# A graph layer with a feed-forward stage: neighbour sums in one burst per block, four groups of 32 nodes side by side, and every sixth product on VectorE

## The chip, the cores and the metric

The kernel runs on 1 core of one Trainium2 chip. The time is the device time of one execution in microseconds (us), from launch to the last output. Two runs of the kernel before were timed.

## What is computed

`x` has 6250 nodes of 512 values; `src` and `dst` are 106,250 edges (both directions of 50,000, and one loop for each node), sorted by `dst`. The weights of the feed-forward stage are ternary in groups of 128 with a scale each.

```
xn  = layernorm(x)
agg = segment_sum(xn[src], dst, 6250)
h   = xn @ W_self + b_self + (agg / max(deg, 1)) @ W_neigh
h   = layernorm(h) * gamma + beta
h   = where(h >= 0, h, alpha * h)
x1  = x + h + xn
x1n = layernorm(x1)
hid = silu(x1n @ wq_gate.T) * (x1n @ wq_up.T)      # wq: ternary, scale per group of 128
out = x1 + hid @ wq_down.T
```

## The kernel before

Nodes are taken in 49 blocks of 128. There are two stages.

**Prologue.** For each block ScalarE normalises `x`, TensorE turns it (`turn0`) and multiplies it with W_neigh (`product`), and the result is stored to a table in HBM as two fp16 halves, 2 KB a node. Beside this the ternary weights are made (VectorE compares, POOL subtracts, L737), and the range of edges of each block is found on VectorE (`edge_ranges`, with large `hit` tiles and a reduction over partitions on POOL), spread over the blocks from `RANGES_FROM` = 9 on.

**Main stage.** A hand-written schedule of slots, one for each block, and 18 ticks in each. In slot t:
- POOL gathers the table rows of the edges of block t: 18 indirect DMAs (`STEPS`), each 128 edges, 256 KB, into a ring `rows` of 18 tiles (L759). A tile is free again when its sum has run (`p_used`).
- VectorE builds `hot`, a matrix of ones for edge against node for 18 x 128 edges and 128 nodes (L1293), and counts edges per node from it (L1303, three reductions).
- TensorE sums: for each of the 18 tiles two matmuls of 512 columns (`sum_step`: L889 and L891, high and low half) with `hot` as the weights, into `agg_ps`. The table `AGG_AT` spreads them over ticks 2 to 17, between the matmuls of the feed-forward stage. `degree` (L877, one column) runs at tick 6.
- VectorE and ScalarE finish the block: mean, two layer norms, slope (`norms`, in slots t+1 and t+2); SyncE turns it by DMA for the feed-forward stage.

**Feed-forward work** runs in the same slots. Blocks are taken in chunks: one block, then 12 chunks of 4 blocks (512 columns). A step is one group of 128 inputs: two matmuls (L994, L995, high and low half) into one of 6 banks `f_ps`. Because each group has its own scale, the bank is multiplied in place by a ratio between two steps of one sum (a "product", L1088 on ScalarE, L1432 on VectorE). The six banks take turns. A chunk of four blocks has 132 steps and 106 products. `own` steps (x @ W_self in fp32, L807, four for each of the later blocks) stand in the same list and weigh two steps each. `PACE` says how many steps go into a slot: 38, and 35 (`EVEN`) in the last 11 slots. A chunk does not start before its last block is ready: chunk c at slot 4c + 3.07. Before slot 49 all products are ScalarE's; after it VectorE takes two of five.

In the first five slots 23 blocks more are multiplied by W_self (`held_part`), each with a load and a store of 256 KB.

Each engine runs its list in order. What an instruction waits for holds everything behind it on that engine.

Of the kernel before, what the change touches and what calls it, by code (L numbers as in the profile page):

```python
# [23 lines left out]
PER_LOAD = 2  # L24
LOADS = STEPS // PER_LOAD
TICKS = 18
BIG = float(1 << 17)
# [9 lines left out]
def build(nc, x, src, dst, W_self, b_self, W_neigh, gamma, beta, alpha, w_gate, w_up, w_down, out):  # L37
# [8 lines left out]
    PASS = STEPS * P  # L46
    EP = 125
# [57 lines left out]
    PACE, EVEN = 38.0, 35.0  # L105
# [62 lines left out]
    AGG_AT = [[] for _ in range(TICKS)]  # L168
    for j in range(STEPS):
        AGG_AT[2 + j * (TICKS - 2) // STEPS].append(j)  # L170

# [36 lines left out]
    room = [(t, k) for t in range(BLOCKS + 8) for k in ((12, 17) if t < BLOCKS else (2, 11))]  # L208
# [53 lines left out]
    src_pad = nc.dram_tensor("src_pad", (E + PASS,), I32, kind="Internal").ap()  # L262
    dst_pad = nc.dram_tensor("dst_pad", (E + PASS,), F32, kind="Internal").ap()

    with ExitStack() as ctx:
# [9 lines left out]
        rows = sb("rows", [P, STEPS, 2 * D], F16)  # L275
# [9 lines left out]
        hot = sb("hot", [P, 2, P, STEPS], F16)  # L285
        node_j = sb("node_j", [P, P, STEPS], F16)
# [4 lines left out]
        idx = sb("idx", [P, 2, STEPS], I32)  # L291
        dstv = sb("dstv", [P, 2, STEPS], F32)
        dstl = sb("dstl", [P, STEPS], F16)
        identf = sb("identf", [P, P], F32)
        ident = sb("ident", [P, P], F16)
# [6 lines left out]
        top = sb("top", [P, BLOCKS], F32)  # L302
        st6p = sb("st6p", [P, 6], F32)
# [12 lines left out]
        rangem = sb("rangem", [P, 2 * BLOCKS], F32)  # L316
        rangei = sb("rangei", [P, 4 * BLOCKS + 1], I32)
        most = sb("most", [P, 1], F32)
        padi = sb("padi", [P, STEPS], I32)
# [10 lines left out]
        idx_o = sb("idx_o", [P, STEPS], I32)  # L330
        dstv_o = sb("dstv_o", [P, STEPS], F32)
# [9 lines left out]
        at = list(np.cumsum([0, 4 * NSEG, NSEG, 2 * BLOCKS, 3 * NG]))  # L341
        segs, posi, ranges, rscl = (x1[:, 10, int(lo):int(hi)] for lo, hi in zip(at, at[1:]))
        segs, posi, rscl = segs.rearrange("p (a b) -> p a b", b=NSEG), posi.bitcast(I32), rscl.rearrange("p (a b) -> p a b", b=NG)
# [10 lines left out]
        YR = 6  # L354
        ystage = [work16[:, i] for i in range(3)] + [hsxflat[:, i * D:(i + 2) * D] for i in (8, 10)] + [x1[:, X1R - 1].bitcast(F16)]
# [12 lines left out]
        hotflat = hot[:, :, :, :].rearrange("p a b c -> p (a b c)").bitcast(F32)  # L368
# [425 lines left out]
        def _(pe):  # L794
# [16 lines left out]
            for i in range(BLOCKS):  # L811
# [10 lines left out]
                if i == 0:  # L822
                    turn0(1)
# [776 lines left out]
```

## Time and profile before

| | us |
|---|---|
| median of two timed runs | 1696.73 |
| the two runs | 1694.02 and 1699.44 |
| span of the profiled execution | 1674.1 |
| TensorE matmul busy | 1537.9 (92%) |
| VectorE, ScalarE, POOL busy | 1055.9, 1177.1, 938.3 |

The span runs from the first to the last instruction of the profiled execution; what lies around it makes up the difference to the timed runs, 22.6 us against the median. The slices of the page show three parts: the prologue to about 205 us, the main stage to about 1550, and a tail in which only feed-forward work is left. Matmuls are pipelined, so the busy time of TensorE says little alone; the distance from one start to the next does. Durations of ScalarE and VectorE instructions overlap a little in the same way.

### The profile page before, as it was taken

How to read it: one execution, taken by the hardware profiler on the slowest of the kernel's cores; microseconds unless marked ns; L12 is line 12 of the kernel's file. 1: busy time of each engine (PE TensorE's matmuls, PEld its weight loads, DVE VectorE, ACT ScalarE, POOL GpSimd, SP SyncE). 2: the span in 40 equal slices, each digit the busy share in tenths (PEclk: the TensorE clock that was granted, in tenths of full speed). 3: DMA queues.
4: the chain of work that ended last, by engine and by line, in shares of the span. 5: the costliest groups of instructions: out<-in, count | busy, mean ns of one | idle time of the engine just before them, and what ended most of it. 6: DMA issues, size and time to landing. Idle time of an engine off the chain costs nothing.

```text
span 1674.1 us, 21796 instructions
## 1 busy us (share of the span) xinstructions
PE 1537.9 (92%) x6421; PEld 750.7 (45%) x6422; DVE 1055.9 (63%) x2305; ACT 1177.1 (70%) x2248; POOL 938.3 (56%) x936
## 2 busy tenths in 40 slices
PE   7999989987889999999999998999998998989897
PEld 3444434444444454444444444444444443444343
DVE  8999624655565565564665756557466466573876
ACT  5577500026777787778787786869887887879796
POOL 2123277666676666666666766667666666764000
PEclk9999989989998999999999999999999999999999
DMA  9869488997776887777777867787777777784101
GB/s 303 257 219 292 125 293 313 274 282 208 213 226 189 225 224 221 218 229 210 216 212 226 228 201 230 209 235 211 217 209 223 218 213 223 206 228 129 38 14 37
DMA packets 210883, 353.40 MB, mean 211 GB/s; under 512 B 105482, under 2 KB 105482, under 8 KB 210754
## 3 DMA queue, kind: packets, MB, share of 16 engines
q0 software_dynamic: 70560, 231.27, 47.4%
q1 hardware_dynamic: 140204, 120.73, 24.5%
q8 instruction: 52, 0.85, 0.2%
q14 instruction: 67, 0.55, 0.1%
HBM read 295.79 MB, written 39.62 MB: 200 GB/s over the span
## 4 chain that ended last, share of the span: by engine, by line
PE 84%; issue 6%; ACT 6%; DVE 2%; DMA 1%; another core or an unknown queue 0%; DVEq 0%; SPq 0%; ACTq 0%
PE f_ps L994 21%; PE f_ps L995 20%; PE f_ps L807 20%; PE agg_ps L889 10%; PE agg_ps L891 10%; ACT f_ps L1088 4%; PE side_ps L934 1%; PE agg_ps L803 1%; PE side_ps L803 1%; PE f_ps L889 0%; PE f_ps L891 0%; ACT hT L1113 0%; ACT acc L1098 0%; DVE acc L1440 0%; DMA rows<-in_x 0%
## 5 line engine op out<-in xcount | busy, mean ns | idle before, releaser
L759 POOL DMA_INDIRECT rows<-node_table,idx x882 | 891.6, 1011 | 442.6 <-issue 241.3
L1088 ACT ACTIVATE f_ps<-f_ps,ratio 128x512 f32<-128x512 f32 (+2 forms) x1303 | 777.0, 666 | 240.6 <-PE f_ps L995 163.2
L994 PE MATMUL f_ps<-x1T,tern 128*128 128x512 f16 (+2 forms) x1144 | 424.2, 374 | 52.0 <-issue 28.2
L995 PE MATMUL f_ps<-x1T,tern 128*128 128x512 f16 (+2 forms) x1144 | 422.4, 372 | 0.0
L889 PE MATMUL agg_ps<-rows,hot 128*128 128x512 f16 x846 | 328.5, 388 | 22.8 <-issue 22.8
L891 PE MATMUL agg_ps<-rows,hot 128*128 128x512 f16 x846 | 326.1, 385 | 4.3 <-issue 4.3
L1440 DVE SCALAR_TENSOR_TENSOR acc<-f_ps,scl,acc 128x512 f32<-128x512 f32 (+2 forms) x143 | 102.4, 717 | 229.0 <-PE f_ps L995 116.4
L994 PE MATMUL f_ps<-hT,tern 128*128 128x512 f16 (+2 forms) x572 | 213.4, 376 | 25.6 <-issue 13.0
L995 PE MATMUL f_ps<-hT,tern 128*128 128x512 f16 (+2 forms) x572 | 212.6, 374 | 0.0
L994 PEld LDWEIGHTS f_ps<-x1T,tern 128*128 128x128 f16 x1144 | 113.1, 99 | 216.6 <-issue 67.2
L889 PEld LDWEIGHTS agg_ps<-rows,hot 128*128 128x128 f16 x846 | 120.1, 142 | 133.3 <-issue 64.2
L995 PEld LDWEIGHTS f_ps<-x1T,tern 128*128 128x128 f16 x1144 | 113.9, 100 | 109.6 <-issue 7.1
L891 PEld LDWEIGHTS agg_ps<-rows,hot 128*128 128x128 f16 x846 | 121.6, 144 | 84.0 <-issue 39.9
L1453 DVE TENSOR_TENSOR hT<-acc,hT 128x512 f16<-128x512 f32 (+2 forms) x143 | 93.5, 654 | 84.9 <-issue 47.1
L1303 DVE TENSOR_REDUCE degs<-hot 128x44 f16<-128x792 f16 x147 | 133.1, 944 | 0.0
L1098 ACT ACTIVATE acc<-f_ps,scl 128x512 f32<-128x512 f32 (+2 forms) x143 | 98.4, 693 | 28.7 <-PE f_ps L995 23.1
L807 PE MATMUL f_ps<-wself,xj 128*128 128x512 f32 x208 | 107.3, 597 | 2.9 <-issue 1.7
L994 PEld LDWEIGHTS f_ps<-hT,tern 128*128 128x128 f16 x572 | 56.7, 99 | 116.1 <-ACT f_ps L1088 39.9
L737 POOL TENSOR_TENSOR hsx<-hsx 128x512 f16<-128x512 f16 x33 | 38.7, 1175 | 102.5 <-DVE hsx L1266 58.9
L1129 ACT ACTIVATE work<-x,nmn,rsn 128x512 f32<-128x512 f32 x49 | 41.6, 849 | 74.4 <-issue 54.0
L1113 ACT ACTIVATE hT<-acc 128x512 f16<-128x512 f32 (+2 forms) x143 | 90.3, 631 | 2.7 <-DVE acc L1440 2.4
L995 PEld LDWEIGHTS f_ps<-hT,tern 128*128 128x128 f16 x572 | 57.2, 100 | 55.4 <-issue 4.9
(176 smaller groups left out, 1705.1 us busy)
## 6 DMA issues: line engine op xcount, KB each, us to landing
rows<-node_table,idx POOLq DMA_INDIRECT x882
hsx<-own_rows SPq DMA_DIRECT2D x49, 256.0 KB
hsx<-in_x SPq DMA_DIRECT2D x48, 256.0 KB
out_nodes<-work SPq DMA_DIRECT2D x48, 256.0 KB, 2.2
xj<-xnt_rows SPq DMA_DIRECT2D x26, 256.0 KB
node_table<-work SPq DMA_DIRECT2D x25, 256.0 KB, 3.1
acc<-own_rows SPq DMA_DIRECT2D x23, 256.0 KB
own_rows<-acc SPq DMA_DIRECT2D x23, 256.0 KB
```

Source lines behind the costliest of these rows:

```text
L759: pool.indirect_dma_start(out=rows[:, j, :], out_offset=None, in_=table[:, :], in_offset=bass.IndirectOffsetOnAxis(ap=of[:, j:j + 1], axis ...
L807: return pe.matmul(to[:, :], turned_rows[:, k, :], weight[:, k, :], start=(k == 0), stop=(k == KT - 1), skip_group_check=True)
L889: pe.matmul(agg[:, :], hot[:, b % 2, :, j], rows[:, j, 0:D], start=(j == 0), stop=False, skip_group_check=True)
L891: mm = pe.matmul(agg[:, :], hot[:, b % 2, :, j], rows[:, j, D:2 * D], start=False, stop=(j == STEPS - 1), skip_group_check=True)
L994: pe.matmul(to, lhs, parts[0], start=g == 0, stop=False, skip_group_check=True)
L995: pe.matmul(to, lhs, parts[1], start=False, stop=True, skip_group_check=True).then_inc(p_ff, 1)
L1088: act.activation(ps, ps, ACT.Copy, scale=ratio[:, w if up else 2, j:j + 1]).then_inc(a_scaled, 1)
L1098: act.activation(acc[:, 0, u % 2, 0:width], ps, ACT.Silu, scale=scl[:, 0, j:j + 1]).then_inc(a_silu, 1)
L1113: act.activation(hT[:, 0, f, 0:width], acc[:, 1, u % 2, 0:width], ACT.Copy).then_inc(a_hi, 1)
L1303: dve.tensor_reduce(degs[:, lo:hi], hot[:, b % 2, lo:hi, :], AX.X, ALU.add).then_inc(v_degs, 1)
L1440: dve.scalar_tensor_tensor(out=acc[:, 1, u % 2, 0:width], in0=ps, scalar=scl[:, 1, j:j + 1], in1=acc[:, 0, u % 2, 0:width], op0=ALU.mult, ...
L1453: dve.tensor_tensor(hT[:, 1, f, 0:width], acc[:, 1, u % 2, 0:width], hT[:, 0, f, 0:width], ALU.subtract).then_inc(v_hlo, 1)
```

## The change

**Sums.** The 36 matmuls of 128 weight columns, spread over the slot, become one run of 54 matmuls of 32 weight columns at the end of the slot (`sum_block`). Edges are sorted by node, so the 32 nodes of quarter q have their edges in at most seven neighbouring tiles, tile 4q - 1 to 4q + 5. Round i (0 to 6) takes tile 4q - 1 + i for each quarter; the four matmuls of a round write partitions 0-31, 32-63, 64-95 and 96-127 of `agg_ps`. Seven rounds of two halves with four quarters, less the two of tile -1, are 54.

```diff
-    def sum_step(b, j):
...
-        if j % PER_LOAD == 0:
-            pe.wait_ge(gathered[j // PER_LOAD], (b + 1) * 16 * PER_LOAD)
-        pe.matmul(agg[:, :], hot[:, b % 2, :, j], rows[:, j, 0:D], start=(j == 0), stop=False,
...
-        mm = pe.matmul(agg[:, :], hot[:, b % 2, :, j], rows[:, j, D:2 * D], start=False, stop=(j == STEPS - 1),
...
-        if j % PER_LOAD == PER_LOAD - 1:
-            mm.then_inc(p_used, 1)
...
+    FREE_AFTER = (2, 4, 6)
...
+    def sum_block(b):
+        pe.wait_ge(v_hot, b + 1)
+        pe.wait_ge(v_inv, b + 1)
+        pe.wait_ge(v_idx, 2 * min(b + 3, BLOCKS))
+        for i in range(WINDOW):
+            of_round = [q for q in range(QUARTERS) if tile_of(q, i) >= 0]
+            pairs = max(tile_of(q, i) for q in of_round) // 2 + 1
+            for n in range(waited, pairs):
+                pe.wait_ge(gathered[pair % (RING // 2)], 32 * (pair // (RING // 2) + 1))
+            for part in range(2):
+                for q in of_round:
+                    lo = q * QN
+                    mm = pe.matmul(agg_ps[lo:lo + QN, :], hot[:, b % 2, i, lo:lo + QN],
+                                   rows[:, (b * STEPS + tile_of(q, i)) % RING, part * D:(part + 1) * D],
...
+            if i in FREE_AFTER:
+                mm.then_inc(p_used, 1)
```

**Ring.** `rows` has 22 tiles in place of 18. POOL may be four gathers ahead of the block being summed; the other 14 wait for rounds 2, 4 and 6 of the sums before.

```diff
-                for load in range(LOADS):
-                    after(pool, p_used, (b - 1) * LOADS + load + 1 if b else 0)
-                    gather_load(idx[:, b % 2], load, gathered[load])
+                for j in range(STEPS):
+                    g = b * STEPS + j
+                    if g % 2 == 0 and g >= RING:
+                        pool.wait_ge(p_used, used_count((g - RING) // 2))
+                    gather(g % RING, idx[:, b % 4, j:j + 1], gathered[g % RING // 2])
```

**Edge lists.** They are loaded as 18 rows of 128, turned by TensorE (`turn_edges`, one 128-column matmul per block at tick 6) and copied to `idx` and `dstl` by VectorE at tick 9 (`take_edges`). `hot` has 8 x 128 elements per partition in place of 18 x 128, and the three counting reductions become one.

**Schedule.** `PACE` 38 becomes 42, `EVEN` 35 becomes 39. VectorE takes every sixth product before slot 49.

```diff
-    PACE, EVEN = 38.0, 35.0
+    PACE, EVEN = 42.0, 39.0
-            by = False if SLOT_OF[s] < BLOCKS else products % 5 in (1, 3)
+            by = products % 6 == 3 if SLOT_OF[s] < BLOCKS else products % 5 in (1, 3)
```

**Prologue.** The ranges of edges are found otherwise: POOL converts `dst` and `src` and compares 50 x 196 elements per partition (`count_segments`, at block 9), TensorE adds over the partitions with 50 matmuls of 196 columns and 5 of 170 after the product of block 23, and VectorE works out the ranges in small instructions at block 25. The large `hit` operations on VectorE and the POOL reduction go. POOL also waits for all weights (`v_scl`) before its first gather.

```diff
+                if i == RANGES_FROM + 14:
+                    pe.wait_ge(pool_counts, 1)
+                    for n in range(NSEG):
+                        pe.matmul(first_ps[:, 0:NQ], onesm[0:EP, :], hit[:, n, :], start=(n == 0), stop=(n == NSEG - 1))
```

The list of TensorE in one slot in the middle of the main stage, before: `degree` (L877) and what follows it; `agg_ps` is the sum, the `f_ps` rows are feed-forward.

```order
L877 MATMUL side_ps<-ones,degs 128x1
L889 MATMUL agg_ps<-rows,hot 128x512
L891 MATMUL agg_ps<-rows,hot 128x512
L994 MATMUL f_ps<-x1T,tern 128x512
L995 MATMUL f_ps<-x1T,tern 128x512
L994 MATMUL f_ps<-x1T,tern 128x512
L995 MATMUL f_ps<-x1T,tern 128x512
L889 MATMUL agg_ps<-rows,hot 128x512
L891 MATMUL agg_ps<-rows,hot 128x512
L807 MATMUL f_ps<-wself,xj 128x512
```

The same list of the change, around the end of such a slot:

```order
L1067 MATMUL f_ps<-x1T,tern 128x512
L1068 MATMUL f_ps<-x1T,tern 128x512
L1067 MATMUL f_ps<-x1T,tern 128x512
L1068 MATMUL f_ps<-x1T,tern 128x512
L968 MATMUL agg_ps<-rows,hot 32x512 x54
L1067 MATMUL f_ps<-x1T,tern 128x512
L1068 MATMUL f_ps<-x1T,tern 128x512
```

The sums no longer stand between feed-forward steps; these follow each other without a break, and all 54 matmuls of the sum come after them.

VectorE in one slot before, from the ones matrix `hot` and the counts `degs` on:

```order
L1290 TENSOR_SCALAR dstl<-dstv,base_m 128x18
L1293 TENSOR_TENSOR hot<-dstl,node_j 128x2304
L1398 TENSOR_SCALAR inv<-side_ps,osc 128x1
L1400 RECIPROCAL inv<-inv 128x1
L1458 SCALAR_TENSOR_TENSOR hsx<-work,hsx 128x512
L1303 TENSOR_REDUCE degs<-hot 128x44 x2
L1303 TENSOR_REDUCE degs<-hot 128x40
L1534 SCALAR_TENSOR_TENSOR hsx<-work,neg_alpha,hsx 128x512
```

The same place of the change; L1501 is a product in place on a feed-forward bank:

```order
L1361 TENSOR_TENSOR hot<-dstl,node_j 128x1024
L1467 TENSOR_SCALAR inv<-agg_ps,osc 128x1
L1469 RECIPROCAL inv<-inv 128x1
L1353 CAST idx<-agg_ps 128x18
L1354 TENSOR_SCALAR dstl<-agg_ps,base_m 128x18
L1522 TENSOR_TENSOR hT<-acc,hT 128x512
L1501 TENSOR_SCALAR f_ps<-f_ps,ratio 128x512
L1527 SCALAR_TENSOR_TENSOR hsx<-work,hsx 128x512
L1490 TENSOR_TENSOR work<-side_ps,x 128x512
L1369 TENSOR_REDUCE degs<-hot 128x128
L1602 SCALAR_TENSOR_TENSOR hsx<-work,neg_alpha,hsx 128x512
```

`hot` and `degs` are smaller, two reads of the turned edge lists have come, and products of the feed-forward stage stand among the norms.

## Rows read from the trace of the kernel before

**Rows 1.** Busy time of each engine by stretch: TensorE, loads, VectorE, ScalarE, POOL, clock, DMA
```profile
core 0: us, PE busy (x) PEld busy (x) DVE busy (x) ACT busy (x) POOL busy (x), PEclk, DMA share, GB/s
0.00:205.00 205.00, 195.26 (x594) 95.79 (x596) 181.12 (x417) 131.95 (x412) 46.63 (x54) 1.00 0.81 242
317.00:345.00 28.00, 27.96 (x87) 14.10 (x86) 16.83 (x38) 4.74 (x7) 19.51 (x20) 1.00 0.98 305
457.00:1549.00 1092.00, 1014.83 (x4425) 492.55 (x4424) 659.69 (x1442) 874.04 (x1483) 722.05 (x713) 0.98 0.75 214
1549.00:1674.00 125.00, 109.32 (x524) 51.08 (x522) 95.22 (x164) 97.87 (x166) 0.00 (x0) 0.96 0.09 30
```

**Rows 2.** Chain that ended last, prologue, pieces in order of time: start, us
```profile
188.00 3.44 PE f_ps L807 x8
...
191.87 3.44 PE f_ps L807 x8
```

**Rows 3.** Timeline of TensorE, main stage: start us, us, instruction
```profile
845.34 0.38 PE L889 MATMUL agg_ps<-rows,hot 128*128 128x512 f16 x1
845.55 0.38 PE L891 MATMUL agg_ps<-rows,hot 128*128 128x512 f16 x1
845.77 0.38 PE L994 MATMUL f_ps<-hT,tern 128*128 128x512 f16 x1
```

**Rows 4.** The same view, matmuls of the one-block chunk, 128 columns
```profile
406.15 0.22 PE L994 MATMUL f_ps<-x1T,tern 128*128 128x128 f16 x1
406.21 0.22 PE L995 MATMUL f_ps<-x1T,tern 128*128 128x128 f16 x1
```

**Rows 5.** The same view, the `degree` matmuls of slots 1 and 7
```profile
255.54 0.17 PE L877 MATMUL side_ps<-ones,degs 128*128 128x1 f16 x1
424.08 0.17 PE L877 MATMUL side_ps<-ones,degs 128*128 128x1 f16 x1
```

**Rows 6.** Line L877: ns min/median/max, first and last start us
```profile
L877 PE MATMUL side_ps<-ones,degs x49: 167/167/211, 205.9 to 1536.2; 128*128 128x1 f16 x49
```

**Rows 7.** Costliest groups: busy us, mean ns, idle before and what ended it
```profile
L759 POOL DMA_INDIRECT rows<-node_table,idx x882 | 891.6, 1011 | 442.6 <-issue 241.3
L889 PE MATMUL agg_ps<-rows,hot 128*128 128x512 f16 x846 | 328.5, 388 | 22.8 <-issue 22.8
L891 PEld LDWEIGHTS agg_ps<-rows,hot 128*128 128x128 f16 x846 | 121.6, 144 | 84.0 <-issue 39.9
L1303 DVE TENSOR_REDUCE degs<-hot 128x44 f16<-128x792 f16 x147 | 133.1, 944 | 0.0
```

**Rows 8.** Timeline of POOL, gathers without and with a wait
```profile
801.75 0.95 POOL L759 DMA_INDIRECT rows<-node_table,idx  x1 [2.94 <-PE agg_ps L891]
803.01 0.94 POOL L759 DMA_INDIRECT rows<-node_table,idx  x1 [0.30 <-issue]
```

**Rows 9.** DMA issues: KB each, median us to landing; first a queue's packets, MB, share
```profile
q0 software_dynamic: 70560, 231.27, 47.4%
out_nodes<-work SPq DMA_DIRECT2D x48, 256.0 KB, 2.2
xnt_rows<-work SPq DMA_DIRECT2D x13, 256.0 KB, 5.0
acc<-own_rows SPq DMA_DIRECT2D x23, 256.0 KB
```

**Rows 10.** Timeline of ScalarE, main stage
```profile
844.17 5.30 ACT L1088 ACTIVATE f_ps<-f_ps,ratio 128x512 f32<-128x512 f32 x9
```

**Rows 11.** Groups by shape, VectorE, main stage or all
```profile
L1293 DVE TENSOR_TENSOR hot<-dstl,node_j 128x2304 f16<-128x2304 f16 x49 | 66.9, 1365 | 1.7
L1432 DVE TENSOR_SCALAR f_ps<-f_ps,ratio 128x512 f32<-128x512 f32 x33 | 24.5, 753 | 3.1 <-PE f_ps L995 2.6
```

**Rows 12.** Line L737, the POOL subtraction in the prologue; then its timeline
```profile
L737 POOL TENSOR_TENSOR hsx<-hsx x33: 1142/1156/1496, 30.1 to 195.5; 128x512 f16<-128x512 f16 x33
61.91 1.16 POOL L737 TENSOR_TENSOR hsx<-hsx 128x512 f16<-128x512 f16 x1 [4.92 <-DMA tern<-hsx]
```

More of the change, by code:

```diff
@@ L592, in overflow @@
                             end = sp.value_load(rangei[0:1, bass.ds(b + BLOCKS, 1)], min_val=0, max_val=E)
-                            with sp.Fori(first, end, PASS) as at:
+                            with sp.Fori(first, end, OPASS) as at:
                                 n = sp.snap(passes)
@@ L755, in _, with gather @@
                 pool.wait_ge(st_xt[i], 16 * len(range(i, len(LATER), XTR)))
-            def gather_load(of, load, s):
-                for j in range(load * PER_LOAD, (load + 1) * PER_LOAD):
-                    pool.indirect_dma_start(
-                        out=rows[:, j, :], out_offset=None, in_=table[:, :],
-                        in_offset=bass.IndirectOffsetOnAxis(ap=of[:, j:j + 1], axis=0)).then_inc(s, 16)
+            def gather(at, of, s):
+                pool.indirect_dma_start(
+                    out=rows[:, at, :], out_offset=None, in_=table[:, :],
+                    in_offset=bass.IndirectOffsetOnAxis(ap=of, axis=0)).then_inc(s, 16)
             def overflow():
@@ L776, in overflow @@
                                 pool.sem_inc(pool_turn, 1)
-                                for load in range(LOADS):
-                                    gather_load(idx_o, load, o_rows)
+                                for j in range(OSTEPS):
+                                    gather(j, idx_o[:, j:j + 1], o_rows)
                                 pool.reg_add(passes, passes, 1)
@@ L843, in overflow @@
                                       skip_group_check=True)
[L844 removed]
+                            with pe.Fori(0, beyond, OPASS):
                                 n = pe.snap(passes)
                                 pe.wait_ge(o_hot, n + 1)
[L847 to L849 removed]
+                                pe.wait_ge(o_rows, n * (16 * OSTEPS) + 16 * OSTEPS)
+                                for j in range(OSTEPS):
+                                    pe.matmul(own_ps[:, 0:1], hot[:, 1, j, :], ones[:, 0:1], start=False, stop=False,
                                               skip_group_check=True)
                                     for part in range(2):
[L852 removed]
+                                        mm = pe.matmul(agg_ps[:, :], hot[:, 1, j, :], rows[:, j, part * D:(part + 1) * D],
                                                        start=False, stop=False, skip_group_check=True)
@@ L1344, in _ @@
                 if i == BLOCKS - 1:
-                    for _ in count_edges(0):
-                        pass
+                    count_edges(0)
                 if i == 36:
```

397 lines of the change are left out of this document (221 added, 176 removed).

## Prediction

> **What bounds the kernel now.** I read the stretches first, then the chain, then the timelines of the engines that come near it. In the prologue TensorE is the chain: one block every 3.87 us (188.00 to 191.87), of which 3.44 are the product and the rest the turning [rows 2]. In the main stage TensorE is busy 1014.8 of 1092 us, ScalarE 874.0, POOL 722.1, VectorE 659.7, and the DMA engines 0.75 [rows 1]. In the first slots DMA is the limit: 0.98 busy at 305 GB/s [rows 1]. The tail, 125 us from 1549, is feed-forward work alone [rows 1].
>
> The length of a slot is the distance of the `degree` matmuls: 205.9 to 1536.2 for 49 [rows 6], with slot 1 at 255.5 and slot 7 at 424.1 [rows 5]. So slots 1 to 6 take 168.5 us together, and the 41 intervals after slot 7 take 1112.1, 27.1 each. The work of TensorE in such a slot: a matmul of 512 columns starts every 0.216 us (845.34 to 845.77 is two) [rows 3]. The sums are 36 x 0.216 = 7.8 us. A chunk of four blocks has 132 steps, and the `own` steps count as about 17 more, so 149 x 0.432 = 64.4 us in four slots, 16.1 each. Turning back, degree and small things I put at 0.6. That is 24.5; the other 2.6 us are waits and half clock (the granted clock averages 0.98 [rows 1]).
>
> **Sums.** 36 starts go, 54 of 32 columns come. The trace has no 32-column matmul, so their cost S is bounded from both sides. Below: if the four quarters of a half round stream together, 14 x 0.216 = 3.0 us; weights and matmul together cannot be started faster than the pairs of the one-block chunk, 0.055 us apart (406.15 to 406.21) [rows 4], and 54 x 0.055 = 3.0 says the same. Above: if nothing overlaps, 54 x 0.216 = 11.7 us. I take 4.3: the lower bound, 0.06 us per half round for four weight loads that are short beside the 0.144 us of a full one [rows 7], and 0.2 us at either end. So 3.5 us leave TensorE in each slot. The Trainium skill ("TensorE: Matmul & The Clock Gate", Part 3) gives 2.38 times for three such matmuls side by side; as an estimate, the same share of the ideal for four makes S 3.7. No row here shows it. The same section speaks against the change: weight loads pass running matmuls only in another row group, and all these share the rows; that is the third rival.
>
> **The pace.** At 42 units a slot the 149 units of a chunk fill three slots with 42 x 0.432 = 18.1 us and leave 23 units, 10 us, for the fourth, because a chunk may not start earlier. From slot 38 on (39 units) a heavy slot has 16.8 us; the `own` steps have run out by then, and 132 - 117 = 15 units, 6.5 us, are left for the fourth. Heavy slot: 18.1 + 4.3 + 0.75 (0.6, turned edges and the degree's switch) + waits. I keep 3.0 us of waits, a little more than today: the six banks come round every 2.6 us where sums between them stretched this to 3.9. A ScalarE product takes 5.30 / 9 = 0.59 us [rows 10]; today ScalarE has 874.0 / 1092 x 27.1 = 21.7 us in a slot. One product in six goes (26.5 per block, so 4.4 x 0.59 = 2.6 us), which leaves 19.1 on average, some 20.5 in a heavy slot. It can no longer work much while the sums run, so it is nearly full during the 18.1. Sum 26.1 for a heavy slot; 24.9 at 39 units, 24.6 with the slot after a light one, which starts a tick late.
>
> **VectorE.** It gives up 2 x 0.944 of the three counts [rows 7] (2304 elements become 1024), some 0.5 of the 1.365 for `hot` [rows 11], and takes 4.4 x 0.753 = 3.3 [rows 11] and about 0.4 for the edge lists. From 659.7 / 1092 x 27.1 = 16.4 it goes to about 17.7 of 25. Not a bound, but its queue is fuller, and a product behind a chain of norms holds a bank. The cover is the 3.0 us of waits above.
>
> **POOL and the light slot.** A gather takes 1.011 us [rows 7] plus 0.30 to the next [rows 8]: 18 x 1.31 = 23.6 us a slot, under 26.1. In a light slot TensorE has only 10 + 4.3 + 0.75, and the ring decides: 14 gathers start after round 2 of the sums before, the last 13 x 1.31 = 17.0 us later, and lands after some 3.3 (256 KB rows have 2.2 and 5.0 [rows 9]); round 6 needs it, three rounds or 1.8 us behind round 2. That makes 17.0 + 3.3 - 1.8 = 18.5, with some clock lost in the idle time 20.
>
> Slots 7 to 48: 23 heavy x 26.1 = 600, 8 x 24.6 = 197, 10 light x 20 = 200, and one of 20: 1017. Less the last slot, for the same 41 intervals: 993 against 1112, **119 saved**.
>
> **Slots 1 to 6.** In 1 to 4 a slot moves 231.27 / 49 = 4.7 MB of gathers [rows 9], 0.8 of x, own rows and `xj`, and 4.6 held blocks at 0.52: 7.9 MB, at 305 GB/s [rows 1] 25.9 us. This is little under today's 28, so 4 x 26 + 26 + 23 = 153 against 168.5: **15 saved**.
>
> **Prologue.** TensorE does 50 x 196 + 5 x 170 = 10,650 columns more; at 0.055 us for 128 [rows 4] that is 4.6, with the two turned lists **5 lost**, on the chain. POOL's comparison must be ready when TensorE gets to it, at about 118 us. POOL needs 1.156 us for 512 elements [rows 12], 2.3 ns each; 2 x 9800 + 4 x 850 elements are 52 us from about 63 (its last subtraction before is at 61.91 [rows 12]). Ready at 115, just hidden; without that cover every us counts in full. VectorE, 181 of 205 us busy [rows 1], is relieved. The tail has 2 us less work, since the pace is higher.
>
> **Sum.** 1674.1 + 5 - 15 - 119 - 2 = 1543 for the span. The profiled execution lies 22.6 us under the median of the timed runs, so 1696.7 - 131 = **1566**.
>
> **Rivals.**
> - *POOL sets the pace* (15%). If ScalarE's relief ends the waits, a heavy slot falls to the 23.6 of POOL, somewhat less if gathers lose their stretched cases (0.95 + 0.30 alone is 22.5). All slots near 22.8: 42 x 22.8 = 958, 59 less, 1507. For it: ScalarE is today's second load. Against it: the steps are closer together.
> - *Queues of ScalarE and VectorE* (20%). Waits of 5 us in place of 3: 31 x 2 = 62 more, 1628. For it: ScalarE nearly full beside the feed-forward run, and VectorE in the loop for the first time in this stage.
> - *Weight loads not hidden in the sums* (12%). If each half round has to let its matmuls end (0.38 [rows 3]) before new weights count, 14 x 0.48 = 6.7 us. 31 x 2.4 + 10 x 1.2 + 6 = 92 more: 1658.
> - *The four groups run one after another* (7%): the change doesn't do what it says. S = 11.7, heavy slot 33.6, light 25.5, first slots 31. 23 x 7.5 + 8 x 7.5 + 10 x 5.5 + 8 = 295, plus 6 x 5: **1890, slower**. It decides from S = 7.5: there 31 x 3.2 + 10 x 1.5 + 10 use up the 131.
> - *POOL late in the prologue* (3%), twice the 52 us: 1566 + 50 = 1616.
>
> **How the numbers follow.** The forecast case has 43%, with a range of its own of 1535 to 1605. Two in ten are left out by 1505 to 1660: all of the last-group case, half of the loads case, part of either side. A measurement tells about 2% from no change, 34 us: faster is under 1663. That holds for the forecast, POOL, queues, the late POOL, and half of the loads case: 0.85. Same: the other half and a little of the queues, 0.07. Slower 0.08.
>
> **What would show it.** Right: rounds of the sums about 0.6 us apart and a burst of 4 to 4.6 us; three slots near 26 and one near 20 in turn; POOL with waits of 2 to 3 us on TensorE in heavy slots and none in light ones; prologue 5 us longer. Wrong: the burst at 7 us or more; POOL back to back throughout; TensorE's waits ended by VectorE products; a gap of TensorE near 115 us.

## The result and the profile after

| | before | changed |
|---|---|---|
| median of two runs | 1696.73 us (1694.02 to 1699.44) | 2282.87 us (2271.44 to 2294.30) |
| profiled execution, its span | 1674.1 us | 2269.7 us |

The changed kernel takes 1.346 times as long (95% interval 1.329 to 1.363). The forecast was 1566 us, range 1505 to 1660, so it is wrong in sign and far outside its range. The span of the changed kernel's profile lies 1.7 us under the time of the same execution (2269.7 and 2271.44), in the runs below 1.7 to 2.5. So most of the 22.6 us between span and median ahead of the prediction is the difference between two executions, and not what lies around the span.

The costliest groups of the page of the changed kernel (busy us, mean ns | idle before and what ended most of it), to be read against [rows 7]:

```profile
L811 POOL DMA_INDIRECT rows<-node_table,idx x882 | 852.4, 966 | 1046.4 <-PE agg_ps L968 774.0
L1162 ACT ACTIVATE f_ps<-f_ps,ratio 128x512 f32<-128x512 f32 (+2 forms) x1106 | 667.3, 647 | 765.5 <-PE f_ps L1068 394.8
L1067 PE MATMUL f_ps<-x1T,tern 128*128 128x512 f16 (+2 forms) x1144 | 466.8, 412 | 372.7 <-ACT f_ps L1162 153.0
L968 PE MATMUL agg_ps<-rows,hot 128*32 128x512 f16 x2646 | 172.9, 405 | 51.5 <-DVE inv L1469 29.1
L1369 DVE TENSOR_REDUCE degs<-hot 128x128 f16<-128x1024 f16 x49 | 93.6, 1910 | 0.0
```

POOL issued 882 gathers in less busy time than before (852.4 against 891.6), but its idle time before them rose from 442.6 to 1046.4 us. ScalarE waits for TensorE and TensorE for ScalarE: no engine is full. The page's chain says the same, with a new item:

```profile
PE 44%; another core or an unknown queue 18%; DVE 14%; issue 11%; ACT 9%; DMA 2%; SPq 1%; POOL 0%; DVEq 0%; ACTq 0%; POOLq 0%
```

Busy time of each engine in 800 us of the main stage (stretch, length, TensorE, weight loads, VectorE, ScalarE, POOL, granted clock, DMA share, GB/s), against the row of the main stage in [rows 1]:

```profile
450.00:1250.00 800.00, 519.33 (x2674) 191.53 (x2674) 367.56 (x805) 391.86 (x682) 350.04 (x363) 0.78 0.52 149
```

TensorE is busy 65% of the time instead of 93%. The mean granted clock of the stretch is 0.78, where the main stage before had 0.98 (1.00 is 2.4 GHz); TensorE now pauses for 3 to 5 us several times in a slot, as the lines below show. In a slot of 39.6 us it is thus busy for 25.7 and idle for 13.9; before these were 25.2 and 1.9. The burst itself came out as drawn. The timelines of TensorE (start us, us, instruction) and of the `degree` line (ns min/median/max, first and last start us):

```profile
1027.02 3.20 PE L968 MATMUL agg_ps<-rows,hot 128*32 128x512 f16 x54
1036.00 0.38 PE L1068 MATMUL f_ps<-x1T,tern 128*128 128x512 f16 x1
1040.33 2.07 PE L860 MATMUL f_ps<-wself,xj 128*128 128x512 f32 x2 [3.95 <-issue]
...
1048.48 0.63 PE L1068 MATMUL f_ps<-x1T,tern 128*128 128x512 f16 x1
1053.66 1.09 PE L1009 MATMUL side_ps<-identf,yT 128*128 128x128 f32 x4 [4.55 <-issue]
```

```profile
L950 PE MATMUL agg_ps<-ones,degs x49: 163/211/211, 237.8 to 2119.8; 128*128 128x1 f16 x49
```

54 matmuls with 32 columns of weights each in 3.20 us: the four column groups do run side by side. 41 of the 49 bursts take 3.2 to 3.3 us. Yet from one `degree` matmul to the next it is 39.6 us on average over the 41 intervals after slot 7 (27.1 before), and the first one comes at 237.8 instead of 205.9 [rows 6]. By stretches, from the starts of that line:

| stretch of the span | before, us | changed, us | difference |
|---|---|---|---|
| up to the first `degree` | 205.9 | 237.8 | +31.9 |
| slot 0 | 49.7 | 43.7 | -6.0 |
| slots 1 to 6 | 168.5 | 213.3 | +44.8 |
| 41 intervals from slot 7 | 1112.1 | 1625.0 | +512.9 |
| rest | 137.9 | 149.9 | +12.0 |

**What stands in the way in a slot.** POOL's timeline just behind the burst above; the middle line stands for 16 more like it, 1.25 us apart:

```profile
1028.78 0.95 POOL L811 DMA_INDIRECT rows<-node_table,idx  x1 [18.16 <-PE agg_ps L968]
1030.04 0.95 POOL L811 DMA_INDIRECT rows<-node_table,idx  x1 [0.31 <-issue]
...
1050.07 0.94 POOL L811 DMA_INDIRECT rows<-node_table,idx  x1 [0.30 <-issue]
1070.37 0.95 POOL L811 DMA_INDIRECT rows<-node_table,idx  x1 [19.35 <-PE agg_ps L968]
```

ScalarE's timeline in the same microseconds:

```profile
1031.57 3.64 ACT L1162 ACTIVATE f_ps<-f_ps,ratio 128x512 f32<-128x512 f32 x6 [3.51 <-PE f_ps L1068]
1039.57 0.66 ACT L1162 ACTIVATE f_ps<-f_ps,ratio 128x512 f32<-128x512 f32 x1 [4.36 <-remote]
1043.12 0.66 ACT L1162 ACTIVATE f_ps<-f_ps,ratio 128x512 f32<-128x512 f32 x1 [2.89 <-PE f_ps L860]
1047.33 0.69 ACT L1172 ACTIVATE acc<-f_ps,scl 128x512 f32<-128x512 f32 x1 [3.55 <-remote]
...
1054.41 0.69 ACT L1172 ACTIVATE acc<-f_ps,scl 128x512 f32<-128x512 f32 x1 [5.17 <-remote]
```

TensorE starts no feed-forward matmul between 1048.48 and 1054.54, so what ScalarE reads at 1054.41 was finished by 1049.1 at the latest. ScalarE stood idle for 5.17 us all the same; in the chain this very time is `1049.24 5.19 another core or an unknown queue`. It moves when the last gather, issued at 1050.07, has had some 4 us. The signal (the update of a semaphore, a counter that the other engine waits for) that the matmul has finished got to ScalarE late, and because ScalarE then frees the bank late, TensorE stopped too (3.95, 4.55 us).

This holds over the whole trace. The table takes each ScalarE product that found ScalarE idle, and gives the time from the start of its second matmul to the start of the product, by how many gathers POOL had started in an unbroken row (starts less than 1.7 us apart) when that matmul started (no gather near: none from 1.7 us before that start to the start of the product). Medians in us, cases in parentheses:

| kernel, run | no gather near | 0 to 2 | 3 to 5 | 6 to 8 | 9 and more |
|---|---|---|---|---|---|
| before | 0.41 (39) | 1.20 (34) | 2.46 (86) | 3.22 (69) | 3.49 (11) |
| changed | 0.42 (78) | 1.70 (64) | 4.46 (142) | 12.61 (89) | 13.24 (14) |
| before, e5 | 0.41 (38) | 0.42 (19) | 0.42 (25) | 0.42 (31) | 0.42 (99) |
| changed, e6 | 0.41 (34) | 0.42 (16) | 0.42 (15) | 0.42 (21) | 0.42 (42) |
| burst in the kernel before, e16 | 0.41 (40) | 9.00 (7) | 0.42 (31) | 4.94 (196) | 12.80 (55) |
| changed and paced, e14 | 0.41 (37) | 1.27 (57) | 0.67 (37) | 3.58 (34) | 3.74 (8) |
| changed with plain transfers, e12 | 0.42 (68) | 0.42 (3) | 0.42 (41) | 0.42 (12) | 0.42 (8) |

The recorded updates of the semaphores say the same and show whose they are: 21% of those of TensorE's matmuls come more than 1 us after the end of the matmul in the changed kernel, 13% in the kernel before, and 0.3 to 0.4% in e5, e6 and e12. Of ScalarE's updates it is 1% or less in every one of these runs.

The kernel before has the effect too. Half of its gathers stand in rows of 8 or fewer there (in e5, where nothing is late, the median is 21); in the changed kernel the median gather stands in a row of 18, and 44 rows of 12 or more hold 773 of the 882.

**The prologue.** VectorE's timeline (three lines), POOL's (two), TensorE's (one):

```profile
66.93 0.75 DVE L1276 SCALAR_TENSOR_TENSOR work<-f_ps,osc,work 128x512 f16<-128x512 f32 x1 [2.30 <-ACT work L1121]
...
72.40 9.03 DVE L1246 TENSOR_SCALAR tmp<-mv 128x7 f32<-128x7 f32 x1
83.95 23.91 DVE L1257 SCALAR_TENSOR_TENSOR nmr<-mv,rstd 128x7 f32<-128x7 f32 x1
64.74 16.66 POOL L786 TENSOR_TENSOR tern<-x,rows 125x9800 f16<-125x9800 f32 x1
83.86 24.97 POOL L790 TENSOR_SCALAR tern<-tern 125x9800 f16<-125x9800 f16 x1
108.67 5.22 PE L860 MATMUL f_ps<-acc,x1T 128*128 128x512 f32 x8 [18.90 <-DVE hsx L1276]
```

A VectorE step on 128x7 elements is recorded with 23.91 us and ends within 1 us of the end of POOL's comparison; the other, of 9.03, ends with POOL's subtraction. A VectorE step with one of its operands in PSUM (66.93) takes its usual 0.75 us beside the same subtraction. Behind the blocked step stand the VectorE steps that empty TensorE's banks, and TensorE waits for them.

Up to the first `degree` the 31.9 us are thus made up, by TensorE's idle times and the distances of its starts: 18.9 for this wait, 3.3 for one at 51.4 us on ScalarE, 4.9 for the added matmuls (forecast 5), and 4.9 because matmuls that both kernels have took longer: the first eight behind the long wait take 5.22 us, 3.60 elsewhere.

### The profile page after: what moved, and what is told of

Its sections match the earlier page's. It is cut to its first block, busy times and chain, and to the rows that moved or that the text cites. A ratio compares the mean times of both kernels' runs of the same rounds, so it can differ in the third digit from the quotient of the medians.

```text
span 2269.7 us, 23912 instructions
## 1 busy us (share of the span) xinstructions
PE 1545.3 (68%) x7407; PEld 605.8 (27%) x7408; DVE 1146.1 (50%) x2453; ACT 1088.7 (48%) x2051; POOL 941.8 (41%) x944
## 3 DMA queue, kind: packets, MB, share of 16 engines
q0 software_dynamic: 70560, 231.27, 35.1%
## 4 chain that ended last, share of the span: by engine, by line
PE 44%; another core or an unknown queue 18%; DVE 14%; issue 11%; ACT 9%; DMA 2%; SPq 1%; POOL 0%; DVEq 0%; ACTq 0%; POOLq 0%
PE f_ps L1068 13%; PE f_ps L1067 13%; PE f_ps L860 9%; PE agg_ps L968 6%; ACT f_ps L1162 6%; DVE f_ps L1501 1%; DVE degs L1369 1%; DVE acc L1509 1%; DVE hot L1361 1%; DVE nmr L1257 1%; DVE hT L1522 1%; ACT acc L1172 1%; ACT hsx L1192 1%; PE side_ps L1009 1%
## 5 line engine op out<-in xcount | busy, mean ns | idle before, releaser
L811 POOL DMA_INDIRECT rows<-node_table,idx x882 | 852.4, 966 | 1046.4 <-PE agg_ps L968 774.0
L1162 ACT ACTIVATE f_ps<-f_ps,ratio 128x512 f32<-128x512 f32 (+2 forms) x1106 | 667.3, 647 | 765.5 <-PE f_ps L1068 394.8
L1067 PE MATMUL f_ps<-x1T,tern 128*128 128x512 f16 (+2 forms) x1144 | 466.8, 412 | 372.7 <-ACT f_ps L1162 153.0
L1068 PE MATMUL f_ps<-x1T,tern 128*128 128x512 f16 (+2 forms) x1144 | 465.6, 411 | 0.0
L1501 DVE TENSOR_SCALAR f_ps<-f_ps,ratio 128x512 f32<-128x512 f32 (+2 forms) x272 | 196.9, 725 | 503.4 <-PE f_ps L1068 305.1
L1067 PE MATMUL f_ps<-hT,tern 128*128 128x512 f16 (+2 forms) x572 | 243.0, 428 | 196.6 <-ACT f_ps L1162 112.8
L1068 PE MATMUL f_ps<-hT,tern 128*128 128x512 f16 (+2 forms) x572 | 242.6, 427 | 0.0
L968 PE MATMUL agg_ps<-rows,hot 128*32 128x512 f16 x2646 | 172.9, 405 | 51.5 <-DVE inv L1469 29.1
L860 PE MATMUL f_ps<-wself,xj 128*128 128x512 f32 x208 | 131.8, 721 | 18.0 <-issue 8.9
L968 PEld LDWEIGHTS agg_ps<-rows,hot 128*32 128x32 f16 x2646 | 79.8, 101 | 144.9 <-issue 57.7
L1522 DVE TENSOR_TENSOR hT<-acc,hT 128x512 f16<-128x512 f32 (+2 forms) x143 | 92.8, 649 | 24.7 <-issue 17.2
L1369 DVE TENSOR_REDUCE degs<-hot 128x128 f16<-128x1024 f16 x49 | 93.6, 1910 | 0.0
L1543 DVE SCALAR_TENSOR_TENSOR work<-agg_ps,inv,hsx 128x512 f32<-128x512 f32 x49 | 36.7, 749 | 94.8 <-PE agg_ps L968 83.0
L1203 ACT ACTIVATE work<-x,nmn,rsn 128x512 f32<-128x512 f32 x49 | 40.1, 818 | 87.6 <-issue 54.9
```

What stands on the lines that cost most here:

```text
L811: pool.indirect_dma_start(out=rows[:, at, :], out_offset=None, in_=table[:, :], in_offset=bass.IndirectOffsetOnAxis(ap=of, axis=0)).then_i ...
L860: return pe.matmul(to[:, :], turned_rows[:, k, :], weight[:, k, :], start=(k == 0), stop=(k == KT - 1), skip_group_check=True)
L968: mm = pe.matmul(agg_ps[lo:lo + QN, :], hot[:, b % 2, i, lo:lo + QN], rows[:, (b * STEPS + tile_of(q, i)) % RING, part * D:(part + 1) * D] ...
L1067: pe.matmul(to, lhs, parts[0], start=g == 0, stop=False, skip_group_check=True)
L1068: pe.matmul(to, lhs, parts[1], start=False, stop=True, skip_group_check=True).then_inc(p_ff, 1)
L1162: act.activation(ps, ps, ACT.Copy, scale=ratio[:, w if up else 2, j:j + 1]).then_inc(a_scaled, 1)
```

## The experiments

The runs of one group share runs of the kernel before, and this turned out to matter: the kernel before took 1518 to 1523 us beside e1 to e11, e13 and e15, and 1683 beside e12, e14, e16 and e17. Nothing lies between. I call the first timely jobs and the second late jobs; the record, 1697 and 2283, is of the second kind. The figure beside e12 and e14 is the same one, 1683.01. The expectations speak of chips, because I held it for a property of the chip at first; it isn't one, since chip 9 gave 1523 beside e13 and 1683 beside e16. All times below are of single executions.

**e1, paced gathers.** In POOL's loop:

```diff
+            def paced(b, pair):
+                at = (b, 2 * (pair - 2)) if pair >= 2 else (b - 1, 14 + 2 * pair)
+                after(pool, p_ff, sum(1 for of in AT_OF.values() if of < at))
...
                         pool.wait_ge(p_used, used_count((g - RING) // 2))
+                        paced(b, j // 2)
```

> The changed kernel with one edit: POOL no longer issues the 18 gathers of a block in one unbroken row; pair by pair it waits for TensorE's feed-forward count, so that the pairs are spread over the ticks of the slot. Sums, tables and VectorE's share stay. In the changed kernel 35 unbroken rows of 18 gathers stand, and the ScalarE product starts a median 14 us behind its matmul once such a row has gone on for 9 or more, 0.42 us where no gather runs. Theory G (TensorE's signals come late to the other engines while POOL issues gathers without a break; the burst makes the breaks rare): the lateness falls to the 3 to 6 us of the kernel before or less, slots of 38 to 40 us fall to 26 to 32, the time to 1650 to 1950. Theory C (the 32-column matmuls side by side disturb TensorE): no change, 2200 to 2300. Theory V (VectorE's products in place hold the banks): no change, 2200 to 2300.

**e2, the burst in the kernel before.**

```diff
-        AGG_AT[2 + j * (TICKS - 2) // STEPS].append(j)
+        AGG_AT[TICKS - 1].append(j)
```

> The kernel before with one edit: the 18 steps of a block's sum, 36 matmuls of 128 columns, all stand at the end of the slot's last tick rather than spread over the ticks. Ring, tables, pace and engine shares stay. Its ring holds 18 tiles, so POOL cannot run ahead of the burst at all and issues 18 gathers in one row behind each burst. Theory G: the signals come late here too, without any column tiling and without VectorE's products; slots above 35 us, 2000 to 2300 in all. Theory C: only the burst's own length counts and the ring's wait of some 4 us per slot, 1750 to 1900. Theory V: as C.

**e3, no products on VectorE.**

```diff
-            by = products % 6 == 3 if SLOT_OF[s] < BLOCKS else products % 5 in (1, 3)
+            by = False if SLOT_OF[s] < BLOCKS else products % 5 in (1, 3)
```

> The changed kernel with one edit: VectorE takes none of the products before slot 49, ScalarE takes them all, as in the kernel before. Theory G: within 60 us of the changed kernel, 2220 to 2340, a little slower if ScalarE's queue matters. Theory V (a product held behind VectorE's own chain keeps a bank and stalls TensorE): most of the loss comes back, 1650 to 1900.

**e4, plain transfers.**

```diff
-                pool.indirect_dma_start(
-                    out=rows[:, at, :], out_offset=None, in_=table[:, :],
-                    in_offset=bass.IndirectOffsetOnAxis(ap=of, axis=0)).then_inc(s, 16)
+                pool.dma_start(rows[:, at, :], table[at * P:(at + 1) * P, :]).then_inc(s, 16)
```

> The changed kernel with one edit: in place of each indirect gather POOL issues a plain transfer of 128 rows of 2 KB from a fixed place of the same table; count, bytes, order, waits and queue stay. It leaves out the choice of the rows, so the sums are of other rows. Theory G in its narrow form (it is the issuing of indirect gathers that keeps TensorE's signals back): lateness near 0.4 us and slots of 25 to 28 us, 1550 to 1700. Theory M (it is the mass of bytes arriving, or any issue by POOL): lateness and time as in the changed kernel, 2100 to 2300. Theory C: 2100 to 2300.

Measured beside 1520 of the kernel before: e1 1599, e2 1692, e3 1584, e4 1534. Every number is far below 2283, and below what every theory had for it; in all four the lateness is 0.42 in the median and never above 0.67, in rows of any length. So nothing followed for the record before the two kernels themselves had been run there.

**e5 and e6, both kernels again; e7, POOL's count in pieces; e8, e1 and e7 together.** The edit of e7, the same for both long steps:

```diff
-                pool.tensor_scalar(hit, hit, 0.0, None, ALU.is_gt).then_inc(pool_counts, 1)
+                for lo in range(0, NSEG, 5):
+                    mm = pool.tensor_scalar(hit[:, lo:lo + 5], hit[:, lo:lo + 5], 0.0, None, ALU.is_gt)
+                mm.then_inc(pool_counts, 1)
```

> The kernel before, unchanged, profiled in this job. On the chip of e1 to e4 one run of it took 1520 us, 176 less than in the runs shown ahead of the prediction, and in e1 to e3 the ScalarE products start 0.42 us behind their matmul whatever the gathers do. If the late signals belong to some chips, this job shows either about 1520 us with a lateness of 0.42 us, or about 1697 us with medians of 1.3 to 6.5 us in rows of gathers; nothing between. If they are of the kernel, 1697 us.

> The changed kernel, unchanged, beside e5. Where e5 gives 1520 us: theory G+chip (late signals of a chip made the loss of 586 us) says 1560 to 1610, still slower than before, because e3 without VectorE's products gave 1584 and e1 with paced gathers 1599. Where e5 gives 1697 us: 2250 to 2300. A rival, that the burst stalls TensorE by itself on any chip, says above 2000 beside a 1520.

> The changed kernel with one edit: POOL's two long steps of the count (9800 elements each, 16.7 and 25.0 us) are cut into ten pieces each of 980. In the trace of the changed kernel a VectorE step of 128x7 with two operands of SBUF lasts 23.91 us and ends within 1 us of the end of POOL's step of 24.97, another lasts 9.03, and TensorE then waits 18.90 us on VectorE. Theory L (VectorE and POOL exclude each other for the length of one instruction): the longest such VectorE step falls below 3 us, TensorE's wait of 18.9 to below 5, the first degree matmul comes 14 to 19 us earlier, the total is 10 to 19 us less than e6. Rival (POOL's results come too late for TensorE): the gap stays.

> The edits of e1 and e7 together. On a chip with timely signals (e5 at 1520): e1's 1599 less 10 to 19, so 1580 to 1589, and no gain of pacing over e7. On a chip with late signals (e5 at 1697): theory G says 1650 to 1950 where e6 has 2250 to 2300; theory C says no gain, above 2200.

Measured: e5 1519, e6 1567, e7 1550, e8 1585. The same changed kernel takes 2283 us in the record and 1567 in a timely job, 3% above the kernel before. The 800 us of the main stage, e6 first, then e5; then the `degree` line of e7:

```profile
450.00:1250.00 800.00, 701.36 (x4249) 288.11 (x4248) 599.78 (x1282) 622.64 (x1060) 589.28 (x591) 0.97 0.85 243
```
```profile
450.00:1250.00 800.00, 796.35 (x3636) 417.59 (x3635) 538.56 (x1184) 713.62 (x1210) 607.25 (x599) 1.00 0.85 245
```
```profile
L954 PE MATMUL agg_ps<-ones,degs x49: 167/167/167, 216.6 to 1405.6; 128*128 128x1 f16 x49
```

In e5 TensorE is busy in all but 0.5% of this stretch: the kernel before is bound by TensorE alone there. Theory L holds: in e7 the longest VectorE step beside POOL's count is 1.87 us where it was 23.91, TensorE's wait of 18.9 (20.0 in e6) is gone but for 1.7, the first `degree` comes at 216.6 instead of 238.3, and the total falls by 17. In a timely job the pacing of the gathers costs 32 us (e1 beside e6) and 35 (e8 beside e7).

**e9, plain transfers in the kernel before**, by the edit of e4.

> The kernel before with each indirect gather replaced by a plain transfer of 128 rows of 2 KB from a fixed place of the same table, issued by POOL in the same places (the counterpart of e4; it leaves out the choice of the rows). On the chip of e5 to e8 a plain transfer costs POOL 0.54 us where a gather costs 1.25 from start to start. There the 48 intervals between the degree matmuls take 24.4 us each in the kernel before and 24.7 in the changed one, and 18 gathers at 1.25 are 22.5 us. Theory P (on that chip the gathers' issue is the wall of both kernels, so the burst has nothing to give): without it the intervals fall well under 24 here too, to 22.5 to 23.5, 1440 to 1490 in all, where the changed kernel with plain transfers took 1534. Rival (TensorE and ScalarE were the wall of the kernel before): 24 or more stays, 1505 to 1520. On a chip with late signals (the kernel before at 1697): 1530 or less if the indirect gathers keep the signals back, 1650 to 1700 if not.

1514 beside 1518, and 24.07 us an interval after slot 7 where e5 has 24.16: the rival holds, POOL isn't the wall of the kernel before. In the changed kernel the same edit takes 33 us in a timely job (e4 beside e6), and the interval from 24.35 to 23.5.

**e10, the rounds spread; e11, the old pace,** each on top of e7:

```diff
-                if t < BLOCKS:
-                    sum_block(t)
...
+                    if t < BLOCKS and k >= TICKS - WINDOW:
+                        sum_block(t, [k - TICKS + WINDOW])
```
```diff
-    PACE, EVEN = 42.0, 39.0
+    PACE, EVEN = 38.0, 35.0
```

> The kernel of e7 with one edit: the seven rounds of a block's sums no longer stand behind the last tick in one burst, but one in each of the ticks 11 to 17, among the feed-forward matmuls; the column groups, the ring of 22 and its three points of release stay. On a chip with timely signals (the kernel before at 1520): in e6 TensorE is idle before the sums for 40 us of 800 (transfers 18.1, VectorE 12.3 and 9.7) and its clock averages 0.96; the spread rounds wait earlier and with feed-forward work around them. Theory B (what the changed kernel loses in this stage are the burst's own waits): slots of 24.3 fall to 23.3 or less, 1500 to 1525. Rival (the pace and its uneven slots): 1545 to 1560. On a chip with late signals (the kernel before at 1697): the rows of gathers break earlier, the lateness falls in step with their length, 1700 to 2100.

> The kernel of e7 with one edit: the pace of the feed-forward steps goes back to 38 and 35 units a slot. On a chip with timely signals: the slots of 20, 23, 25 and 28 us in turn become even; by the steps alone 149 units are 64.4 us in four slots and with 3.2 of burst, 0.75 and TensorE's idle 1.5 nearly 21.6 are possible, but POOL needs 22.5 for 18 gathers; so 22.8 to 23.8 a slot, 1490 to 1535, if the unevenness costs; 1545 to 1560 if it doesn't. On a chip with late signals theory G expects no gain from it: 2200 to 2290.

e10 1546, e11 1535, beside 1521. Spreading brings 4 us, the old pace 15; neither reaches the kernel before. Intervals: 24.16 and 24.09, against 24.41 in e7, both longer than theory B and the expectation of e11 had them; theory B falls.

**e12, e11 with plain transfers,** by the edit of e4.

> The kernel of e11 with plain transfers in place of the indirect gathers, as in e4 (it leaves out the choice of the rows). In e11 the intervals are 24.04 us each from slot 7 on; its gathers start 1.31 us apart where they aren't held up, 18 x 1.31 = 23.6, and POOL waits for TensorE only 19.5 us of 800. Theory P (POOL's issue is the wall of e11, so the columns saved on TensorE can't be used on a chip with timely signals): without it 22.0 to 23.0 us a slot, 1440 to 1490 in all. Rival (the chain of VectorE and the transfers' bandwidth is the wall): 23.5 or more, 1510 to 1535. On a chip with late signals (the kernel before at 1697): if the indirect gathers keep the signals back, lateness 0.42 us and 1500 to 1600; if any issue by POOL does, 2000 to 2290.

1482, beside 1683: a late job, as it came out, and less than the 1500 to 1600 expected for one. POOL's group between 450 and 1250 us:

```profile
L815 POOL DMA_DIRECT2D rows<-node_table x626 | 330.4, 536 | 470.3 <-PE agg_ps L970 460.3 <-issue 9.9
```

Two things follow. Plain transfers in a late job, in the same queue, with the same 70,560 packets and 231.27 MB, cause no lateness: it comes with the indirect gathers and not with the bytes. That this job was late rests on the one run of the kernel before beside it. And without their cost on POOL the interval is 23.0 us, against 24.1 in e11, where POOL waited for TensorE only 19.5 of 800 us: there POOL's gathers (18 x 1.31 = 23.6 us) were the floor. The plain transfers also kept the DMA engines less busy (42.9% of 1480 us against 52.9% of 1533), so part of the 1.1 us may be theirs; no run here separates the two.

**e13, e11 paced.**

> The kernel of e11 (changed kernel, POOL's count in pieces, pace 38 and 35) with the gathers spread over the ticks of the slot as in e1. The chips differ: on those of e1 to e11 the kernel before takes 1519 to 1523 us and ScalarE starts 0.42 us behind TensorE's matmul whatever POOL does; the record's chip gave 1697, the changed kernel 2283, and lateness that grew with the length of an unbroken row of indirect gathers. On a chip of the second kind (the kernel before at 1680 to 1700) theory G, that these rows keep TensorE's signals back, says: rows of at most 6, median lateness 1 to 3 us, slots of 26 to 31, 1620 to 1850. Rival D, that on such a chip the lateness goes by the load of the DMA engines or by POOL's share of time, not by unbroken rows: slots near 39 as in the changed kernel, above 2100. On a chip of the first kind: 1545 to 1580, as e8 stood to e7.

A timely job, 1548 beside 1523.

**e14, e1 again.**

> The kernel of e1 once more: the changed kernel with the gathers spread over the ticks and nothing else. It stands here for a chip of the record's kind (the kernel before at 1680 to 1700, the changed kernel at 2283). There theory G says: median lateness 1 to 3 us, slots of 26 to 32, 1650 to 1900. Rival D (load, not unbroken rows): above 2100. On a chip with timely signals (the kernel before at 1520) it repeats e1: 1590 to 1605.

A late job: 1758 beside 1683. The same kernel but for the pacing has 2283 beside 1697.

```profile
L811 POOL DMA_INDIRECT rows<-node_table,idx x882 | 890.0, 1009 | 507.2 <-issue 222.9
```
```profile
450.00:1250.00 800.00, 650.52 (x3705) 253.45 (x3704) 520.32 (x1126) 538.47 (x925) 515.59 (x512) 0.94 0.75 211
```

POOL's idle time before the gathers is 507.2 instead of 1046.4 us, though it now waits at more places; the median gather stands in a row of 7; the lateness is about that of the kernel before; an interval is 28.2 us instead of 39.6. Theory G holds. Rival D falls: the load of the DMA engines rose from 0.52 to 0.75 and POOL's busy time from 351.2 to 515.6 of 800 us while the lateness fell. To give POOL more places to wait at made the kernel 525 us faster.

**e15 and e16, e2 again.**

> The kernel of e2 once more (the kernel before with all 36 matmuls of a block's sum at the end of the slot, without column groups and without products on VectorE), for a chip of the record's kind. On a chip with timely signals it took 1692 beside 1520, and 14 of its rows of gathers were 18 long. Where the kernel before takes 1680 to 1700: theory G says long rows and late signals as in the changed kernel, so well beyond the same 172 us more: 1950 to 2300. Rival C (on such a chip it takes the 32-column matmuls or VectorE's share): 1850 to 1890, the 172 us and nothing else.

> The kernel of e2 and e15 once more, for a chip of the record's kind; e15 landed on one with timely signals (1690 beside 1519). Where the kernel before takes 1680 to 1700: theory G 1950 to 2300 (the burst alone makes long rows and late signals), rival C 1850 to 1890 (only the 172 us that it costs on any chip). On a chip with timely signals 1685 to 1695.

e15 was timely, 1690 beside 1519. e16 was late: 2265 beside 1683. Its `degree` line, and the waits of POOL in e16 and in e2 (engine, line, waited for: us in total, times, longest us):

```profile
L877 PE MATMUL side_ps<-ones,degs x49: 167/211/211, 206.1 to 2112.9; 128*128 128x1 f16 x49
```

```profile
POOL rows L759 <- PE agg_ps L891: 786.8, 49, 22.6
```
```profile
POOL rows L759 <- PE agg_ps L891: 197.0, 51, 8.3
```

Timely the burst costs the kernel before 172 us (171 in e15), late 583. e16 has neither column groups nor VectorE's products, nor the new prologue, and its interval is 40.1 us. So the burst alone is enough for a loss like that of the record (586 us); rival C falls. That it works through the rows of gathers that it lets go at once is shown by e14, which keeps the burst and breaks the rows.

**e17, all that helped, together** (e1, e7, e10, e11).

> All that helped one of the kernels, together: the changed kernel with POOL's count in pieces (e7), pace 38 and 35 (e11), the rounds spread over the ticks 11 to 17 (e10), and the gathers paced (e1). On a chip with timely signals: e13's 1548 less what spreading brings (4 in e10), 1538 to 1550, no gain over the kernel before. On a chip of the record's kind e14's 1757, less 22 for the prologue, less 1 to 2 us in each of 48 slots: 1640 to 1700, level with the kernel before at best.

A late job, 1757 beside 1683: no better than e14, outside what I expected. The prologue is 20 us shorter and slots 1 to 6 are 13, but the interval is 28.8 instead of 28.2, 27 us in 41; which of the four edits costs that is not shown. No version found here beats the kernel before in either kind of job with the gathers kept.

## Why the prediction was wrong, point by point

- **The step that failed** is "I keep 3.0 us of waits, a little more than today". I read 2.6 of the 27.1 us of a slot as "waits and half clock" without asking what they were. They go with TensorE's late signals: in e5, where these are missing, the same kernel needs 24.2 us. And I carried them over as a constant where they grow with the length of POOL's rows, which the burst stretches from 8 to 18 (medians). For the interval this gave 24.2 (993 / 41); the record has 39.6. Of these 13.9 us are idle time of TensorE, where I had 3.0 of waits; and its busy time didn't fall with the columns saved (25.7 for 25.2), while in e6, at a mean clock of 0.97, it is 21.3 (701.36 of 800 us). The lower clock behind the pauses (a matmul takes 0.63 us at 1048.48, 0.38 at 1036.00) takes back what the sums gave.
- **How it closes into a circle.** The burst frees its tiles within 3 us; POOL sends 18 gathers in one row of 22 us (1028.78 to 1051); meanwhile the signals come late, the six banks stay full, and TensorE does little; only when the row has ended does it go through the rest of the slot's feed-forward work, to the next burst, for which POOL waits 19.35 us. The two parts of a slot that should lie beside each other lie one behind the other. The kernel before frees one pair after another between feed-forward steps, so in a late job its rows break when POOL has to wait for the next pair.
- **Heavy and light slots.** Forecast 26.1 and 20 in turn, POOL waiting 2 to 3 us for TensorE. In the record POOL waits 16.5 us (774.0 in 47 waits). In e6, without lateness, the slots do differ in turn (means of every fourth from slot 7 to 38: 21.4, 24.4, 24.7, 26.8), and the mean of the 41 intervals is 24.35, against 24.2 forecast. The 1567 of e6 meets my 1566 by luck: 27 us too little for the prologue, 11 too much for slots 1 to 6 (142.3 where I had 153), 6 too much for slot 0, some 12 too little for the rest, so 22 too little for the span (1543, measured 1565); the 22.6 us between span and median, of which e6 has 1.7, make up for it. And the forecast was made from late rows.
- **Sums.** 4.3 us forecast, 3.2 measured; in e6 some 1.2 us of waits come ahead of the rounds. Rounds start 0.43 us apart, where I had 0.6. The rivals on serial groups and on loads not hidden fall: in the burst at 1027.02 the first four matmuls start within 0.02 us, and the weight loads of the next four run beside them, although all use the same 128 rows. What the prediction cites against the change does not hold here. The estimate of 3.7 made with the Trainium skill's figure was 0.5 us too high.
- **VectorE and ScalarE.** 17.7 of 25 us forecast for VectorE, 599.78 / 800 x 24.35 = 18.3 in e6; 19.1 and 19.0 for ScalarE. But two terms were off: the `degs` reduction was to save 2 x 0.944 us and saved 2.83 - 1.91 = 0.9 (it now reads its 1024 elements across the rows of the tile, but no run tests whether that is why); `hot` went from 1.365 to 1.22, not down by 0.5. The share of VectorE pays: e3 without it is 18 us slower than e6. The rival on queues falls.
- **Even in a timely job there was little to win.** TensorE gives up its columns (busy 796 before, 701 after, of 800 us), but POOL's 23.6 us a slot stand right behind the 24.2. I had named this rival (*POOL sets the pace*) and priced it against 26.1. e12 bears it out: 23.0 with plain transfers. e9 shows that before the change it didn't bind.
- **Prologue.** +5 forecast, +31.9 measured, of which e7 gives back 21.7. I had POOL's own time right (47.5 us from 61.4, 52 forecast; ready at 109, 115 forecast), and "just hidden" was wrong: TensorE never waited for POOL's result, but VectorE was held up by POOL's work. The signs of being wrong had "a gap of TensorE near 115 us"; it came at 89.8 to 108.7. The trace of after agrees with a rule of the Trainium skill that I didn't weigh ("SBUF — State Buffer", "Who interferes with whom"): a VectorE instruction with two inputs in SBUF and a GpSimd one that reads SBUF exclude each other, and the later one blocks fully. The step of 23.91 us reads `mv` and `rstd`. The step of 9.03 has one input, so the rule as put here does not cover it. What else the 31.9 are made of stands with the lines of the prologue above.
- **Tail.** -2 forecast, +12.0 in the record and +4.8 in e6. The cause stays open.

## What to carry to other kernels

When a trace shows small waits that a sum doesn't explain, find out what they are before carrying them into a forecast: compare the start of the consumer with the end of its producer, with and without what else runs. The trace of before had the sign already, idle times ended by "remote" in a program on one core, 96.6 us of POOL's alone. Work that is freed in bursts makes its consumer run in bursts, so ask of each resource that is released at once what a long unbroken row of the released work does to the others. Cut a long POOL step into pieces when VectorE has short steps on the path.

## What the runs showed of the hardware that was not expected

- In some jobs TensorE's signals reach ScalarE, VectorE and POOL late while POOL issues indirect gathers of 128 x 2 KB back to back: for ScalarE's products medians of 1.2 to 13 us, rising with the row in both kernels, and 0.42 us when no gather runs. In others, with the same kernels and rows of up to 95 gathers (e5), it is 0.42 throughout and never above 0.67. Chip 9 showed both. With plain transfers of the same size it is 0.42 beside a late run of the kernel before (e12). What makes a job late, and by which path a gather delays the signal, stays open; that the burst and the length of the rows make the loss is shown by e14 and e16, one execution each.
- It makes 1.11 of time for the kernel before (1683 against 1519) and 1.46 for the changed one (2283 against 1567), so such a change can't be judged from one kind of job.
- 54 matmuls with 32 columns of weights each and 512 columns moved take 3.2 us in four column groups that share all 128 rows, 3.6 times less than 54 x 0.216 = 11.7.
- A VectorE step on 128x7 elements lasted 23.91 us beside one long POOL step, and at most 1.87 us beside the same work in ten pieces.
